# Layer 2's attention maxima in batches of 16 chunks instead of 32, with the projection's products ending 32 chunks before the last

## What is computed

```
z = jnp.einsum('ni,hif->nhf', h, W)          # h: normalized x, 2500 x 1024; z: 2500 x 4 x 256
el = jnp.einsum('nhf,hf->nh', z, a_l)
er = jnp.einsum('nhf,hf->nh', z, a_r)
e = jax.nn.leaky_relu(el[src] + er[dst], NEG_SLOPE)
m = jax.ops.segment_max(e, dst, num_segments=N)
ex = jnp.exp(e - m[dst])
s = jax.ops.segment_sum(ex, dst, num_segments=N)
alpha = ex / s[dst]
out = jax.ops.segment_sum(alpha[:, :, None] * z[src], dst, num_segments=N)
```

## Time and profile before

| | us |
|---|---|
| median of 3 runs | 3577.93 (3573.08 to 3578.49) |
| the profiled execution, its own time | 3581.93 |
| its span in the trace | 3580.2 |
| second phase: first product of z to the last maximum | 1557.5 to 2048.5 |
| of it, the chunks, from the first batch's transposes on | 1603.3 to 2048.5 |

### The profile page before, as it was taken

How to read it: one execution, slowest core, us unless ns; L and a number is a source line. 1 busy time by engine, 2 the same in 40 slices (tenths; PEclk the granted TensorE clock), 3 DMA queues, 4 the chain that set the end, 5 groups by cost and what they waited for, 6 DMA issues and landing times. The chain is left out here.

```text
span 3580.2 us, 50457 instructions
## 1 busy us (share of the span) xinstructions
PE 2847.5 (80%) x13602; PEld 2228.0 (62%) x13602; DVE 2455.1 (69%) x5351; ACT 1536.9 (43%) x3068; POOL 1714.2 (48%) x1564
## 2 busy tenths in 40 slices
PE   0996102999996777889899899999999699289996
PEld 0885101444443665877777588888887688278886
DVE  6222602999997665527777799999999564467774
ACT  1221000333333765523333377777776332055554
POOL 4777873666664221247777344444443111023332
PEclk9998555999998898579999899999999688599999
DMA  3333306999997011101111188887877332289997
GB/s 103 79 96 109 92 2 246 353 349 351 348 347 225 30 41 55 40 20 20 26 20 26 38 263 259 262 261 260 260 261 230 114 139 106 103 239 284 282 284 181
DMA packets 223841, 609.09 MB, mean 170 GB/s; under 512 B 47387, under 2 KB 85650, under 8 KB 223582
## 3 DMA queue, kind: packets, MB, share of 16 engines
q0 software_dynamic: 139008, 429.63, 38.7%
q1 hardware_dynamic: 84702, 177.85, 14.5%
HBM read 521.91 MB, written 85.11 MB: 170 GB/s over the span
## 5 line engine op out<-in xcount | busy, mean ns | idle before, releaser
L640 POOL DMA_INDIRECT g_rows<-z_rows,edge_src x704 | 700.4, 995 | 615.6 <-PE g_totals L1397 307.8
L705 PE MATMUL g_sums<-g_rows,g_share 128*128 128x512 f32 x704 | 333.0, 595 | 211.3 <-DVE g_goes L746 211.3
L483 POOL DMA_INDIRECT edge_list<-payload,row_i x320 | 402.3, 1257 | 144.1 <-issue 141.3
L691 ACT ACTIVATE g_scaled_hi<-g_rows,edge_weight_sorted 128x1024 fp32r<-128x1024 f32 x176 | 202.6, 1151 | 540.6 <-DMA g_rows<-z_rows,edge_src 505.4
L1051 POOL DMA_INDIRECT shared<-el_rows,edge_src x352 | 334.8, 951 | 178.8 <-issue 107.0
L1390 PE MATMUL g_sums<-g_rows,g_share 128*128 128x256 f32 x1408 | 348.9, 391 | 0.0
L705 PEld LDWEIGHTS g_sums<-g_rows,g_share 128*128 128x128 f32 x704 | 133.5, 190 | 312.3 <-DVE g_goes L746 211.7
L1342 ACT ACTIVATE g_scaled_hi<-g_rows,g_factor 128x256 fp32r<-128x256 f32 x704 | 299.9, 496 | 4.3 <-DMA g_rows<-z_rows,edge_src 3.2
L1466 DVE SCALAR_TENSOR_TENSOR g_scaled_lo<-g_rows,g_factor,g_scaled_hi 128x256 fp32r<-128x256 f32 x704 | 293.4, 479 | 1.1 <-ACT g_scaled_hi L1342 0.9
L1390 PEld LDWEIGHTS g_sums<-g_rows,g_share 128*128 128x128 f32 x1408 | 255.6, 191 | 27.6
L1245 DVE TENSOR_REDUCE t_largest<-t_masked 128x4 f32<-128x512 f32 x352 | 231.9, 685 | 55.7 <-PE t_masked L1117 49.4
(11 more groups left out here) (359 smaller groups left out, 7696.5 us busy)
## 6 DMA issues: line engine op xcount, KB each, us to landing
e_raw<-in_L_ffn_rw_dram SPq DMA_DIRECT2D x56, 1024.0 KB, 7.5
g_rows<-z_rows,edge_src POOLq DMA_INDIRECT x704, 5.7
z_rows<-z_zout SPq DMA_DIRECT2D x20, 512.0 KB, 2.9
x_rows<-x_all SPq DMA_DIRECT2D x20, 512.0 KB, 2.7
z_rows<-t_zout SPq DMA_DIRECT2D x20, 512.0 KB, 2.8
s_x<-x_rows SPq DMA_DIRECT2D x10, 1024.0 KB, 8.9
xn_rows<-s_rows SPq DMA_DIRECT2D x10, 1024.0 KB, 4.1
z_x<-in_x_dram SPq DMA_DIRECT2D x19, 512.0 KB
```

Of the source, the lines that this page charges most:

```text
L483: pool.indirect_dma_start(out=g.lists[k], out_offset=bass.IndirectOffsetOnAxis(ap=row_i[0:EP, c:c + 1], axis=0), in_=payload[0:EP, c, :], ...
L640: pool.indirect_dma_start(out=r.rows[:, slot, :], out_offset=None, in_=table, in_offset=bass.IndirectOffsetOnAxis(ap=g.src[:, i * GT + q:i ...
L705: nc.tensor.matmul(sums[:, k, h, :], share[:, k, :], r.rows[:, k * GT, h * HALF:(h + 1) * HALF], start=True, stop=False)
```

## The change

Two numbers change. A batch becomes 16 chunks (22 batches instead of 11), so that everything done once for a batch is done twice as often on half the scores. And the 800 products are spread over the first 352 - 32 = 320 chunks instead of 352 - 16 = 336: 2.5 products behind each chunk instead of 2.38, and none behind the last 32.

```
-BATCH = 32
+BATCH = 16
 NB = NE // BATCH
 PRODUCTS = 6 * KD
 Z_FIRST = 160
...
     left = NT * PRODUCTS - Z_FIRST
-    spread = NE - BATCH // 2
+    spread = NE - 2 * BATCH
```

## The result

The changed kernel takes 3616.68 us (median; 3609.86 to 3620.81) against 3578.21 (3573.08 to 3578.56): +38.5 us. The ratio is 1.0109, with a 95% interval of 1.0091 to 1.0127. The prediction said 3624, in a range of 3600 to 3645.

What follows compares the result with a forecast made beforehand. The prediction took waits at borders between batches, not gathers, to bound the chunks' stage. Chunks 0 to 319 (+52.1 us), the last 32 (-0.5) and the start (-4.1, -1.4) sum to +46.1: 3577.9 to 3624 us, range 3600 to 3645.

Steps and rivals of the forecast that it cites:

- What bounds the stage: Chunks' stretch: its own order at the borders between batches binds it, not the gathers, which all stay hidden.
- A border is paid anew, in nearly full: Each added batch border: everything is issued again in full, only smaller, with nothing queued on PE or DVE to cover it.
- The size of the border's price: Border between batches: 4.9 us before, 4.7 us after the change, bounds 2.9 and 6.6.
- the sum's first term: Chunks 0 to 319: 20 segments of 23.1 us replace 10 of 40.99 us, +52.1 us.
- DVE's sum: Segment of 16 chunks counted on DVE: chunks, turns, split and 4.5 us of mask waits make 22.7 us.
- The split's size: DVE's two split instructions at 64 elements: near 0.23 and 0.28 us, 0.2 us saved together.
- The last 32 chunks: End of the stage, from copy to last maximum: 34.2 us instead of 34.7, so -0.5 us.
- The start: First batch: scores turned at 1599.2 instead of 1603.27, -4.1 us, and a shorter slow PE spell, -1.4 us.
- The clock: PE's granted clock behind borders: cheap and dear borders mixed as before, 3.1 us without a fall, 5.7 with; chance 0.69.
- The rival in which every border loses it: Rival at the borders: all 20 lose the clock, a segment is 24.1 us on PE, 3644 us; chance 0.15.
- The rival that only PE's work counts: Rival: borders absorbed, eleven more groups of transposes (7 us) nearly cancel the start's -5.5, 3579 us; chance 0.04.
- The signs named ahead: Expected trace signs in the chunks' stretch: batch intervals, PE's and DVE's waits, granted clock, last maximum near 2095.

Runs made afterwards that it cites:

- batch16_alone: Kernel before with batches of 16 only, products still ending 16 chunks before the last: ratio 1.012 in its first run, 3621.33 us (1.0118) when run again.
- The early split: Changed kernel with DVE splitting a batch's scores 8 chunks before the border, PE and ACT as they are: 4002.55 us, ratio 0.997 against the kernel before.
- batch8: Changed kernel with batches of 8 instead of 16, products still ending 32 chunks before the last: 3692.43 us, ratio 1.0317 against the kernel before.
- busy_border: Changed kernel plus six idle PE products, results overwritten, ahead of PE's wait for the split: 3599.38 us, ratio 1.0059 against the kernel before.
- spread32_again: Second run of the kernel before with batches of 32 kept and products ending 32 chunks before the last: 3578.62 us, ratio 1.0004.
- the first set: First session of follow-up runs, on the first four kernels and the kernel before, which took 4013.53 us there.
- spread32_alone: First run of the kernel before with batches of 32 kept and products ending 32 chunks before the last: ratio 1.001, +2.3 us.

## Why the prediction was right, and where it was off

- **What bounds the stage.** Right. At no border does an engine wait for a gather, before or after. In `batch16_alone` the last gather is issued at 2031.6, and behind it, with no gather left to wait for, the batches still follow each other in 22.35 us. The early split takes that to 19.6. The gathers come in as a bound only once the borders are gone.
- **A border is paid anew, in nearly full.** Right, and shown by three batch sizes: 3.6 and 3.7 us for each added batch.
- **The size of the border's price.** Too large: 4.7 us predicted. This is the term of the sum that was mis-sized. It was the 4.9 us of before less 0.2 for the smaller split, with PE's waits for the split as long as before (2.2 us each, 45 in all). They are 35.4 / 21 = 1.7 us, and the distance from the last product to the first mask fell by 0.6 us, from 3.94 to 3.35, and not by 0.2. The missing 0.4 us at 20 borders are 8 of the 12 us by which the sum's first term was too large: +52.1 predicted, 20 x 22.5 - 409.9 = +40 measured. The starts of the batches of 8 and of 16 give the price in another way. In `batch8` the 1st batch starts at 1599.0 and the 41st at 2123.6, 13.1 us each, and 22.5 - 13.1 = 9.4 us for 8 chunks, or 1.17 a chunk, leaves 3.7 us for the border. For 32 chunks this makes 41.3, against 40.99. By it 16 chunks without a border take 18.8 us, and the prediction had 16.8 + 1.8 = 18.6: the pace between borders was right. Why the waits became shorter by more than the split's 0.2 us no run isolates.
- **DVE's sum** gave 22.7, nearer to 22.5, but partly by luck. In it the wait for masks was 4.5 us a batch and measured 82.9 / 22 = 3.8. With that it makes 22.0.
- **The split's size.** Right: the two instructions take 0.22 and 0.26 us at 64 elements, 0.2 us less than at 128. Transposes and copy take what they took (0.61 and 0.57 us).
- **The last 32 chunks** were predicted at 34.2 us and are 2079.3 - 2045.1 = 34.2. **The start** was predicted at -5.5, and the first copy comes 39.0 us after the first gather instead of 42.7: -3.7 at least, with the clock at 1.00 behind it. So the traces' sum is 40.2 - 0.5 - 3.7 = 36.0 us, as the stage shows, and the 38.5 of the medians hold 2 to 3 us more that the traces don't have.
- **The clock.** The forecast kept the mix of before, and the share of falls is much the same: 17 of 21 borders, 7 of 10 before. The price was too high: 5.7 us for a border with a fall and 3.1 for one without, so 2.6 for the fall, where batches of one kind differ by 1.8. The rival in which every border loses it, which the Trainium skill's rule (TensorE: Matmul & The Clock Gate, section "HAM oscillation — how this bites in real kernels") would give, is refuted as a case: four of 21 borders keep 1.00. The Trainium skill's example there has longer waits in each pass than most of these borders. That PE's waits bring the falls is right, as `busy_border` shows by taking 14 of the 17 away, for 15 us.
- **The rival that only PE's work counts**, with 44 added transposes, is refuted: `busy_border` gives PE 126 products more than the change and is 15 us faster.
- **The signs named ahead** came as follows: batches 22.5 us apart (said 23), PE's waits for the split 35.4 us (said 45), DVE's for masks 82.9 (said 90), the granted clock 0.94 from 1603 to 2045 (said below 0.95), the last maximum at 2079 (said 2095, of which 5 us are the earlier start of the stage).

## What to carry to other kernels

A batch's fixed chain (split, transpose, copy, each on another engine) that stands at the border in every engine's order costs its whole latency each time, and halving the batch doubles that; count borders times latency, not instructions. Small batches and an early issue of the chain belong together: the small batch makes its data available early, and only the early chain uses it. Where two engines are both nearly full, test by an experiment what added work on one of them costs, and compare the clock of the two traces before reading the result: `spread32_again` came out equal with three falls less.

## What the runs showed of the hardware

The two waits of PE at a border of the changed kernel, for the split and for the copy, add up to 1.8 to 3.8 us. Behind 17 of the 21 the granted clock fell. The four at which it stayed at 1.00 have 1.8 to 2.2 us, and waits of the same length brought a fall at others, so their length alone doesn't tell which it will be. Idle products in that time left 3 falls instead of 17, and a clock of 0.98 instead of 0.94 over 442 us. Work that is thrown away made the kernel 15 us faster than the change.

In the first set all kernels took some 435 us longer. The time lies in this stage, while the gathers run, and the trace names no wait for it. In the trace of `spread32_alone` PE, DVE and ACT crawl from about 1580 us on, POOL goes on issuing gathers, and after the last gather (2025) all go on at their usual pace:

```profile
core 0: us, PE busy (x) PEld busy (x) DVE busy (x) ACT busy (x) POOL busy (x), PEclk, DMA share, GB/s
1540.00:1580.00 40.00, 34.72 (x150) 30.24 (x149) 7.02 (x13) 7.92 (x12) 15.22 (x16) 0.71 0.06 2
1620.00:1700.00 80.00, 14.79 (x29) 8.20 (x29) 2.13 (x2) 1.60 (x2) 60.50 (x65) 0.52 0.07 2
...
2100.00:2200.00 100.00, 91.65 (x398) 72.25 (x397) 75.24 (x170) 37.11 (x94) 0.00 (x0) 0.97 0.06 22
```

```profile
PE t_z L1094 <- issue: 204.9, 66, 24.9
PE t_masked L1115 <- issue: 160.4, 6, 88.5
```

PE's idle time from 1580 to 2030 is put down to its own issue, for 377 us. What held the engines up meanwhile no run here shows. The second and third set, with the kernel before and three of these kernels again, didn't show the spell. They ran on other chips, so whether it belongs to that chip or to that session is open too.
